# Four batches after the attention heads: three phases over all batches, or one chain per batch in two lanes

## The chip, the cores and the metric

One core of one Trainium2 chip runs the whole program. The metric is the device time of one execution in microseconds; the median of three runs of the kernel before is 2055.33 us (2053.5 to 2062.61). In the text PE is TensorE, DVE is VectorE, ACT is ScalarE, POOL is GpSimd and SP is the engine whose queue issues most DMAs.

## What is computed

The input is x of shape (4, 1024, 128) in float32: four batches of 1024 tokens. Four blocks follow one another, each on a layer-normed x (the norm has no weights):

```
x = x + L0_attn(norm(x))   # 16 heads of 8; a softmax and a second kernel of |S|, Wo, its own norm, + input
x = x + L0_ffn(norm(x))    # softmax gate over 8 experts, weights under 0.1 dropped, dense expert products
x = x + L1_attn(norm(x))   # one causal head of 64
x = x + L1_ffn(norm(x))    # soft decision tree: 255 sigmoids, 256 leaf probabilities, leaf values, Wout
```

L0_attn ends, once the heads' results f are there, with y = f Wo + bo, out = h + ln_w * normed(y) + ln_b, and x + out, where h is the normed x. The tree turns gates g into leaf probabilities level by level: for each of 8 levels every node's value is split into value * g and value - value * g. No block mixes tokens of different batches.

## The kernel before

`build` (L134) calls four functions in order, and each ends with a barrier of its own block, so that none of the next function's instructions starts before all of this one's are through: `attend_heads` (the heads, all four batches), `mix_experts` (y, its norm, the gate and the experts), `attend_causal` and `descend_tree`. x lives in SBUF as 32 tiles of 128 tokens by 128 (`x_res`), eight tiles a batch. Each engine runs its own list of instructions in the written order; semaphores connect them.

`attend_heads` works in slots, one tile of 128 keys of one head a slot, 512 slots in all. Besides, work that belongs to no slot (projections of the next batch, and once `prepare`, which turns and folds the weights of the later blocks) is laid between the slots at fixed places: a generator yields the slot at which its next piece is due, and the class `Beside` places it.

The three later functions go through the four batches with `rounds` (L121), which staggers parts of neighbouring batches by a fixed lead on each engine:

- `mix_experts` (L930): PE turns f and multiplies it by Wo, DVE adds bo (L1075), takes statistics and norms y (L1084), POOL multiplies by ln_w and adds to x (L1063, L1066). DVE norms x again (L1096), PE turns it (L1016), gate logits go through an exp on ACT (L990) and eight small DVE steps. The eight expert products of a tile come as two matmuls of 512 columns (L1032) in two PSUM banks; DVE adds each expert into x, weighted, with one instruction of 128x128 (L1142, 256 of them). Two tiles are taken in turn, so that an instruction waits for the one before the last.
- `attend_causal` (L1157): per tile of 128 queries, PE multiplies q by k (L1360), DVE adds the mask to the diagonal block (L1240), takes the maximum of each row (L1242) and scales it (L1246), ACT takes the exp (L1283), PE turns the weights (L1370), DVE copies them out of PSUM (L1234), PE weighs v (L1380), DVE divides (L1222), PE turns and ACT copies the result (L1278), PE projects it (L1392), DVE adds it to x (L1228). POOL adds the bias bo1 (L1323).
- `descend_tree` (L1411): norm (L896 and L898 on ACT: Ln and Exp; L1457 on DVE), turning (L1524), logits (L1532), sigmoids on ACT (L1498), 16 DVE instructions for the eight levels (L1469 to L1476, up to 128x1024), turning of the leaves (L1543), their copies (L1505), the product with the leaf values (L1549), the update of x (L1483) and the DMA to the output (L1559). POOL adds the bias (L1516).

Each of the three owns all eight PSUM banks while it runs. `take_stats` (L882), `take_rstd` (L893) and `four` (L918) are helpers that they share. The program has ACT load a set of function tables where a function is not in the loaded one; `attend_heads`, `mix_experts` and `attend_causal` load a set with both Ln and Exp by hand at their start, the rest is placed by the compiler.

## Time and profile before

| what | value |
|---|---|
| median of three runs | 2055.33 us |
| the profiled execution, its own time | 2054.09 us |
| its span in the profile | 2052.3 us |
| granted clock of TensorE, mean over the span | 0.933 of full |
| DVE busy | 1738.2 us (85%) |
| ACT busy | 1631.2 us (79%) |
| PE busy | 1578.5 us (77%) |
| POOL busy | 1406.9 us (69%) |
| DMA, mean | 16 GB/s |

The page divides the span into 40 slices of 51 us and gives the busy share of each engine in tenths. ACT and DVE stand at 9 from slice 4 to slice 31; in the last eight ACT has 1 to 4, POOL 0 or 1, and DVE falls from 8 to 5 or 6. The granted clock stands at 9 of 10 or better in the middle and at 7 or 8 in the end. A share is that of an average over stages, so the views that cut the span by stage are to be read beside it. Idle time of an engine is listed with what ended it; what counts is the idle time of the engine on which the end of the stage hangs.

### The profile page before, as it was taken

The page shows a single profiled execution, that of the slowest core. Times are in us where ns is not written, and L with a number is a line of the kernel's source. Part 1 is how long each engine was busy: PE and PEld are TensorE (multiplying, and loading weights), DVE is VectorE, ACT ScalarE, POOL GpSimd, SP SyncE. Part 2 cuts the span into 40 slices and gives each one's busy share as a digit, 9 for nine tenths or more (in the row PEclk, how much of TensorE's full clock was granted, in tenths as well). Part 3 has the DMA queues.
Part 4 walks back from the last instruction along what each step waited for, and adds up shares of the span by engine and source line. Part 5 has one row for each costly group of instructions (what it writes and reads, how often), then busy time and mean ns, then how long its engine had stood idle before and what let it go on. Part 6 is the DMA issues. An engine that isn't in the chain of part 4 may idle for free. (4 is left out here: it accounts for less than half of the span.)

```text
span 2052.3 us, 26693 instructions
## 1 busy us (share of the span) xinstructions
PE 1578.5 (77%) x8579; PEld 562.9 (27%) x8579; DVE 1738.2 (85%) x3742; ACT 1631.2 (79%) x1406; POOL 1406.9 (69%) x962
## 2 busy tenths in 40 slices
PE   2587787777878878778878887778777587899966
PEld 1122222222222222222222222222222144366655
DVE  3889999997999999879999999999998278755556
ACT  2689999998999999989999999999999411122243
POOL 2889889987999989788998989988998001000000
PEclk7799999999999999989999999999999888877788
DMA  4000000001000000010000000000000000000001
GB/s 113 27 28 13 13 14 17 13 13 31 25 13 13 13 16 15 9 40 13 18 13 13 13 15 16 12 13 13 18 13 7 1 0 1 1 1 1 0 1 42
DMA packets 32490, 33.11 MB, mean 16 GB/s; under 512 B 5657, under 2 KB 23136, under 8 KB 32352
## 3 DMA queue, kind: packets, MB, share of 16 engines
q1 hardware_dynamic: 31056, 31.06, 5.0%
q8 instruction: 71, 1.16, 0.2%
q14 instruction: 67, 0.55, 0.1%
q10 hardware_dynamic: 1296, 0.35, 0.1%
HBM read 22.74 MB, written 8.39 MB: 15 GB/s over the span
## 5 line engine op out<-in xcount | busy, mean ns | idle before, releaser
L879 POOL TENSOR_TENSOR sigma_weights<-grown 128x1024 f32<-128x1024 f32 x448 | 845.6, 1893 | 0.0
L792 ACT ACTIVATE tau_weights<-ps_tau 128x1024 f32<-128x1024 f32 x512 | 740.1, 1446 | 29.6 <-PE ps_tau L424 29.5
L573 DVE TENSOR_SCALAR sigma_weights<-ps_sig 128x512 int32<-128x512 int32 x1024 | 693.4, 677 | 81.3 <-PE ps_sig L415 80.3
L852 POOL TENSOR_SCALAR grown<-sigma_weights,kernel_shape 128x1024 f32<-128x1024 f32 x448 | 501.3, 1119 | 196.8 <-DVE sigma_weights L573 196.7
L778 ACT ACTIVATE sigma_weights<-sigma_weights,kernel_shape 128x2048 f32<-128x2048 f32 x256 | 621.0, 2426 | 0.0
L582 DVE TENSOR_TENSOR running_max<-ps_sig,running_max 128x512 f32<-128x512 f32 x896 | 606.0, 676 | 0.0
L787 ACT ACTIVATE sigma_weights<-sigma_weights 128x2048 f32<-128x2048 f32 x256 | 598.4, 2338 | 0.0
L466 PE MATMUL ps_acc<-sigma_weights,v_heads 128*9 128x512 f32 x2048 | 534.6, 601 | 0.0
L466 PE MATMUL ps_acc<-tau_weights,v_heads 128*9 128x512 f32 x2048 | 533.1, 600 | 0.4 <-DVE sums L599 0.3
L424 PE MATMUL ps_tau<-q_operand,k_operand 128*128 128x512 bf16 x1024 | 310.5, 385 | 262.7 <-ACT tau_weights L792 256.2
L415 PE MATMUL ps_sig<-q_operand,k_operand 96*128 96x512 bf16 x1024 | 400.6, 391 | 67.0 <-DVE running_max L582 41.3
L415 PEld LDWEIGHTS ps_sig<-q_operand,k_operand 96*128 96x128 bf16 x1024 | 99.2, 97 | 483.7 <-DVE running_max L582 287.2
L424 PEld LDWEIGHTS ps_tau<-q_operand,k_operand 128*128 128x128 bf16 x1024 | 63.9, 97 | 412.7 <-ACT tau_weights L792 343.7
L1323 POOL TENSOR_TENSOR x_res<-x_res,bo_rows 128x512 f32<-128x512 f32 x8 | 9.9, 1262 | 152.8 <-DVE z_c L1213 152.8
L466 PEld LDWEIGHTS ps_acc<-tau_weights,v_heads 128*9 128x9 f32 x2048 | 54.4, 88 | 193.9 <-issue 165.3
L1063 POOL TENSOR_TENSOR y_normed<-y_normed,ln_w_rows 128x1024 f32<-128x1024 f32 x4 | 9.4, 2342 | 138.0 <-DVE y_normed L1084 138.0
L783 ACT ACTIVATE sigma_weights<-sigma_weights,kernel_shape 128x1024 f32<-128x1024 f32 x64 | 100.6, 1573 | 0.0
L1032 PE MATMUL ps_me<-experts,turned_sb 128*128 128x512 f32 x128 | 74.8, 735 | 21.0 <-DVE x_res L1142 20.8
L586 DVE TENSOR_REDUCE row_max<-ps_misc 128x4 f32<-128x512 f32 x128 | 87.0, 680 | 2.0 <-PE ps_misc L433 2.0
L579 DVE COPY running_max<-ps_sig 128x512 f32<-128x512 f32 x128 | 87.0, 679 | 0.0
L433 PE MATMUL ps_misc<-ident,running_max 128*128 128x128 f32 x512 | 82.7, 286 | 4.1 <-DVE row_max L586 4.0
L1516 POOL TENSOR_TENSOR x_res<-x_res,bout_rows 128x512 f32<-128x512 f32 x8 | 10.0, 1268 | 104.4 <-DVE z_d L1457 104.4
(169 smaller groups left out, 1459.8 us busy)
## 6 DMA issues: line engine op xcount, KB each, us to landing
q_operand<-q_parts SPq DMA_DIRECT2D x192, 48.0 KB
k_operand<-k_parts SPq DMA_DIRECT2D x64, 144.0 KB
q_parts<-parts SPq DMA_DIRECT2D x24, 128.0 KB, 2.3
k_parts<-parts SPq DMA_DIRECT2D x24, 128.0 KB, 2.3
x_res<-in_L_attn_x SPq DMA_DIRECT2D x8, 256.0 KB, 5.3
q_operand<-max_rows SPq DMA_DIRECT2D x128, 2.0 KB
out<-x_res SPq DMA_DIRECT2D x4, 512.0 KB, 3.2
experts<-in_L_ffn_expert_w SPq DMA_DIRECT2D x1, 512.0 KB
```

What stands on the lines that cost most here:

```text
L415: pe.matmul(ps_sig[:, half, :], kop[0:SIGMA_ROWS, slot, keys], qop[0:SIGMA_ROWS, slot, half * HALF:(half + 1) * HALF], start=True, stop=Tr ...
L424: mm = pe.matmul(ps_tau[:, half, :], kop[:, head % SLOTS, of * P:(of + 1) * P], qop[:, head % SLOTS, half * HALF:(half + 1) * HALF], start ...
L466: mm = pe.matmul(ps_acc[32 * q:32 * q + COLS, :], v[:, (of - 1 + kind) % (2 * H), j, :], weights[:, half * HALF:(half + 1) * HALF], start= ...
L573: dve.tensor_scalar(sig[:, g % SIG_RING, cols].bitcast(I32), ps_sig[:, half, :].bitcast(I32), SIGN_OFF, None, ALU.bitwise_and).then_inc(ma ...
L579: dve.tensor_copy(run[:, of, cols], ps_sig[:, half, :]).then_inc(run_ready, 1)
L582: dve.tensor_tensor(run[:, of, cols], ps_sig[:, half, :], run[:, of, cols], ALU.max).then_inc(run_ready, 1)
L778: act.activation(chunk(c), chunk(c), ACT.Ln, bias=shape[:, CHUNK * c // TB % H, 1:2]).then_inc(ln_done, 1)
L783: act.activation(tile, tile, ACT.Square, bias=shape[:, g // TB % H, 0:1]).then_inc(whole_ready, 1)
L787: act.activation(chunk(c), chunk(c), ACT.Exp, scale=-1.0).then_inc(sig_done, 1)
L792: act.activation(tau[:, g % TAU_RING, :], ps_tau[:, :, :].rearrange("p h q -> p (h q)"), ACT.Exp, scale=float(DH) ** -0.5).then_inc(tau_do ...
L852: pool.tensor_scalar(grown[:, g % GROWN_RING, :], sig[:, g % SIG_RING, :], 1.0, shape[:, g // TB % H, 0:1], ALU.mult, ALU.add).then_inc(gr ...
L879: pool.tensor_tensor(sig[:, g % SIG_RING, :], t, t, ALU.mult).then_inc(sq_ready, 1)
```

## The change

The first function stays, with small additions. The three later ones are gone; in their place `finish_batches` writes for each batch b one chain per engine: y and its norm, gate, experts, causal attention, tree, output. Chains of batches 0 and 2 use the buffers and four PSUM banks of lane "even", 1 and 3 those of lane "odd". A chain is a generator that yields the time at which its next piece is due, counted from CHAIN * b = 60 * b; `together` merges the four generators of an engine into one list by due time. The due times decide the order of the instructions alone: nothing waits for a time. A piece that waits for a semaphore holds up what is behind it on its engine, of the other lane too. A use of a bank waits until the use four places earlier in the same lane was read.

Within the chain:

- The bias rows (bo, gate bias, expert biases, bv and bo1, bout) no longer are added by DVE or POOL. They stand as three bf16 parts in one 3-row tensor, and a matmul of ones with them opens the PSUM accumulation. `prepare` in `attend_heads` makes them: eleven small DVE instructions and five on one partition of 1544 elements, and two DMAs.
- Wo is centred over its columns beforehand, so that y has mean zero; the matmul gives y and y * ln_w side by side. ACT squares with a running sum, takes Ln and Exp per four tiles, and DVE adds y * ln_w * rstd to x in one instruction a tile. POOL has nothing to do after the heads.
- The expert updates of a tile follow one another, each waiting for the one before, in banks of their own (16 uses of 512 columns).
- Causal attention: maxima are taken of the scores by DVE (12 reductions), turned and copied as a row by a DMA into row 64 of q (k has ones there); then the scores are made a second time, keys on the partitions, with the maximum subtracted by the matmul; ACT takes 12 exps straight into the weights, so that these need no turning and no copy by DVE. The mask is added by a bf16 matmul. v is multiplied by wo1 beforehand and has a column of ones, so that the product gives the update and the sum of the weights; DVE takes the reciprocal and adds the update to x, one instruction a tile.
- Norms: DVE norms four tiles, ACT the other four (`Identity` with scale and bias).
- Tree: as before, without the bias on POOL. Each batch is stored in two halves.

The load of the table set at the start of the later functions is gone. The diff, cut to what the text speaks of:

```diff
-LATER = 22
+LATER, ROW32 = 17, 5
...
+SCORES = [(i, g) for i in range(TB) for g in range(1 + i // 4)]
+WEIGHTS = [(k, 0) for k in range(4)] + [(k, 1) for k in range(TB)]
+OUTS = [(0, 1), (2, 3), (4, 5, 6), (7,)]
+
+
+LANES, BANKS = 2, 4
+CHAIN = 60.0
...
+def turns():
+
+    names = ["f0", "f1", "y0", "y1", "y2", "y3", "z0", "z1", "gate"]
+    names += [f"e{i}" for i in range(2 * TB)]
+    names += ["c0", "c1", "q0", "k0", "q1", "k1", "v0", "v1"]
+    names += [f"s{i}" for i in range(12)] + ["m"]
+    names += [f"p{i}" for i in range(6)] + ["o0", "o1"] + [f"p{i}" for i in range(6, 12)] + ["o2", "o3"]
+    names += ["d0", "d1", "g0", "g1", "g2", "g3", "l0", "l1", "l2", "l3", "w0", "w1"]
+    return {name: n for n, name in enumerate(names)}
...
+def together(chains):
+
+    due = [(next(pieces), n) for n, pieces in enumerate(chains)]
+    while due:
+        at, n = min(due)
+        due.remove((at, n))
+        later = next(chains[n], None)
+        if later is not None:
+            due.append((later, n))
...
         attend_heads(nc, a, w)
-        mix_experts(nc, w)
-        attend_causal(nc, w)
-        descend_tree(nc, w, out)
+        finish_batches(nc, w, out)
...
+            def prepare(t0):
+                yield t0 + 4
...
+                yield t0 + 9
+                dve.wait_ge(row_step, 5)
+                dve.tensor_copy(rows3[0:1, :], rows32[:, :]).then_inc(split_step, 1)
+                yield t0 + 10
+                dve.wait_ge(split_step, 1)
+                dve.tensor_tensor(rows32[:, :], rows32[:, :], rows3[0:1, :], ALU.subtract).then_inc(split_step, 1)
+                yield t0 + 11
+                dve.wait_ge(split_step, 2)
+                dve.tensor_copy(split[:, 0, :], rows32[:, :]).then_inc(split_step, 1)
+                yield t0 + 12
+                dve.wait_ge(split_step, 3)
+                dve.tensor_tensor(rows32[:, :], rows32[:, :], split[:, 0, :], ALU.subtract).then_inc(split_step, 1)
+                yield t0 + 13
+                dve.wait_ge(split_step, 4)
+                dve.tensor_copy(split[:, 1, :], rows32[:, :]).then_inc(split_step, 1)
...
+class Lane:
...
+        self.banks = [ctx.enter_context(nc.psum_tensor(f"ps_{name}{i}", [P, HALF], F32)) for i in range(BANKS)]
...
+        self.reach = [self.weights[:, 4 * i:4 * i + 4, :].rearrange("p a c -> p (a c)").rearrange("p (t l) -> p t l", t=TB)
+                      for i in range(2)]
+        self.ready = [sem(f"bank{i}_ready") for i in range(BANKS)]
+        self.read = [sem(f"bank{i}_read") for i in range(BANKS)]
...
+def finish_batches(nc, w, out):
...
+                def biased(n, at, cols, row):
+                    pe.matmul(lane.bank(n)[:, at:at + cols], ones3[:, :], rows3[:, row:row + cols], start=True, stop=False)
...
+                for i in range(4):
+                    n = u(f"y{i}")
+                    yield t0 + 1.6 + 1.1 * i
+                    lane.was_read(pe, u(f"f{i // 2}"))
+                    lane.take(pe, n)
+                    for t in (2 * i, 2 * i + 1):
+                        at = t % 2 * 2 * D
+                        biased(n, at, 2 * D, ROW_Y)
+                        mm = pe.matmul(lane.bank(n)[:, at:at + 2 * D], zt[:, t * P:(t + 1) * P], w["woc"][:, :],
+                                       start=False, stop=True)
+                    done(mm, n)
...
+                for i in range(2 * TB):
+                    n, t, half = u(f"e{i}"), i // 2, i % 2
+                    yield t0 + (18.6 + 1.06 * i if i < 4 else expert_time(i - 3) + 0.2)
+                    lane.take(pe, n)
+                    biased(n, 0, HALF, ROW_E + half * HALF)
+                    done(pe.matmul(lane.bank(n)[:, :], zt[:, t * P:(t + 1) * P], w["experts"][:, 4 * half:4 * half + 4, :],
+                                   start=False, stop=True), n)
...
+                for j in range(12):
+                    yield t0 + 72.8 + 1.05 * j + (2.2 if j >= 6 else 0)
+                    weights(j)
+                    if j == 5:
+                        yield t0 + 78.9
+                        weigh(0)
+                        yield t0 + 79.6
+                        weigh(1)
+                yield t0 + 88
+                weigh(2)
+                yield t0 + 92
+                weigh(3)
...
+                def layer_norm(norm, at):
+                    z0 = 3 * r + norm
+                    yield t0 + at
+                    dve.wait_ge(lane.stats_ready, TB * (z0 + 1))
+                    alone(dve, w["dve_passed"])
+                    for t in range(TB):
+                        dve.bn_aggr(lane.mv[:, t, :], lane.stats[:, t, :]).then_inc(lane.mv_ready, 1)
+                    yield t0 + at + 2
+                    dve.wait_ge(lane.rstd_ready, z0 + 1)
+                    dve.scalar_tensor_tensor(out=lane.shift[:, :], in0=lane.mv[:, :, 0], scalar=-1.0, in1=lane.rstd[:, :],
+                                             op0=ALU.mult, op1=ALU.mult).then_inc(lane.shift_ready, 1)
+                    dve.wait_ge(lane.mv_ready, TB * (z0 + 1))
+                    for t in range(4):
+                        ins = dve.tensor_scalar(lane.z[:, t, :], xt(b, t), lane.mv[:, t, 0:1], lane.rstd[:, t:t + 1],
+                                                ALU.subtract, ALU.mult)
+                    ins.then_inc(lane.z_ready[0], 1)
...
+                for i in range(2 * TB):
+                    n, t = u(f"e{i}"), i // 2
+                    for s in range(4):
+                        yield t0 + expert_time(i) + 0.35 * s
+                        e = 4 * (i % 2) + s
+                        if s == 0:
+                            if i == 0:
+                                dve.wait_ge(lane.gate_step, step + 9)
+                            lane.arrived(dve, n)
+                            if i % 2:
+                                lane.was_read(dve, u(f"e{i - 1}"))
+                        else:
+                            dve.wait_ge(lane.e_step, 3 * (2 * TB * r + i) + s)
+                        ins = dve.scalar_tensor_tensor(out=xt(b, t), in0=lane.bank(n)[:, s * D:(s + 1) * D],
+                                                       scalar=lane.weight[:, t, e:e + 1], in1=xt(b, t),
+                                                       op0=ALU.mult, op1=ALU.add)
+                        if s < 3:
+                            ins.then_inc(lane.e_step, 1)
+                        else:
+                            done(ins, n)
+                    if i % 2:
+                        yield t0 + expert_time(i) + 1.45
+                        lane.was_read(dve, n)
+                        stat(t)
...
+                def squares(i):
+                    n = u(f"y{i}")
+                    lane.arrived(act, n)
+                    for t in (2 * i, 2 * i + 1):
+                        centred = lane.bank(n)[:, t % 2 * 2 * D:t % 2 * 2 * D + D]
+                        ins = act.activation(centred, centred, ACT.Square, accum_out=lane.y_sum[:, t:t + 1])
+                    ins.then_inc(lane.sum_ready, 1)
+
+                def take_y_rstd(g):
+                    cols = slice(4 * g, 4 * g + 4)
+                    act.wait_ge(lane.sum_ready, 4 * r + 2 * g + 2)
+                    act.activation(lane.y_ln[:, cols], lane.y_sum[:, cols], ACT.Ln, bias=w["eps"][:, 0:1], scale=1.0 / D)\
+                        .then_inc(lane.yln_ready, 1)
+                    act.wait_ge(lane.yln_ready, 2 * r + g + 1)
+                    act.activation(lane.y_rstd[:, cols], lane.y_ln[:, cols], ACT.Exp, scale=-0.5).then_inc(lane.y_rstd_ready, 1)
...
+                yield from layer_norm(TREE, 96.9)
+                for g in range(2):
+                    yield t0 + 99.8 + 0.8 * g
+                    copy_turned(u(f"d{g}"), g)
+                for i in range(4):
+                    n = u(f"g{i}")
+                    yield t0 + 102.4 + 0.9 * i
+                    lane.arrived(act, n)
+                    done(act.activation(lane.right[:, 2 * i:2 * i + 2, 0:NODES],
+                                        lane.bank(n)[:, :].rearrange("p (t n) -> p t n", t=2)[:, :, 0:NODES], ACT.Sigmoid), n)
...
+            together([chain(b, CHAIN * b) for b in range(B)])
```

## Rows read from the trace of the kernel before

**Rows 1.** The windows view: length, busy us (instructions) of five engines, granted clock, DMA share, GB/s.

```profile
40.00:1619.50 1579.50, 1232.54 (x7088) 330.73 (x7089) 1445.40 (x2695) 1509.32 (x1154) 1357.08 (x920) 0.97 0.06 17
1619.50:1779.80 160.30, 116.14 (x416) 65.14 (x416) 123.63 (x508) 19.70 (x45) 18.75 (x8) 0.81 0.00 1
1779.80:1965.70 185.90, 164.33 (x752) 115.07 (x752) 99.72 (x340) 53.03 (x129) 9.93 (x8) 0.78 0.00 1
1965.70:2052.30 86.60, 54.30 (x288) 44.92 (x288) 55.23 (x168) 38.00 (x58) 9.97 (x8) 0.84 0.09 25
```

**Rows 2.** The windows view of a stretch inside the heads.

```profile
240.00:400.00 160.00, 127.26 (x754) 33.32 (x754) 154.22 (x285) 160.00 (x119) 143.68 (x99) 1.00 0.04 14
```

**Rows 3.** The view of waits after 1619.5: who waited for whom, us, times, longest.

```profile
ACT prob_c L1283 <- DVE shift_c L1246: 34.1, 29, 3.8
...
DVE v_c L1258 <- PE ps_cx L1347: 27.0, 4, 7.1
DVE mixed L1222 <- PE ps_co L1380: 26.7, 11, 3.9
```

**Rows 4.** The view of groups by form after 1619: count, busy us, mean ns, idle.

```profile
L1142 DVE SCALAR_TENSOR_TENSOR x_res<-ps_me,gate_weight,x_res 128x128 f32<-128x128 f32 x256 | 68.3, 341 | 6.5 <-PE ps_me L1032 6.4
...
L1234 DVE COPY prob_t<-ps_ct 128x512 f32<-128x512 f32 x24 | 16.3, 684 | 2.9 <-PE ps_ct L1370 2.9
...
L1505 ACT ACTIVATE reach_t<-ps_dl 128x512 f32<-128x512 f32 x16 | 9.3, 596 | 21.9 <-PE ps_dl L1543 21.8
```

**Rows 5.** The timeline from 1642 to 1650: gate and first expert updates; start, duration, what.

```profile
1642.19 3.51 PE L1022 MATMUL ps_my<-gate,turned_sb 128*128 128x8 f32 x16
...
1648.84 1.40 DVE L1142 SCALAR_TENSOR_TENSOR x_res<-ps_me,gate_weight,x_res 128x128 f32<-128x128 f32 x5
```

**Rows 6.** The timeline from 1965.7 to 1984: norms, table loads, a held level.

```profile
1965.76 1.64 DVE L886 BATCH_NORM_STATS2 stats_d<-x_res 128x6 f32<-128x128 f32 x8 [0.54 <-PEq L1164]
1967.55 0.64 DVE L890 BATCH_NORM_AGGREGATE mv_d<-stats_d 128x2 f32<-128x6 f32 x8
1968.22 0.30 ACT L896 ACTIVATE lnv_d<-mv_d,eps 128x8 f32<-128x8 f32 x1 [4.24 <-DVE mv_d L890]
1968.56 0.21 ACT L898 ACTIVATE rstd_d<-lnv_d 128x8 f32<-128x8 f32 x1
1968.88 2.14 DVE L1457 TENSOR_SCALAR z_d<-x_res,mv_d,rstd_d 128x128 f32<-128x128 f32 x8 [0.69 <-ACT rstd_d L898]
...
1973.30 1.28 ACT L1498 ACT_TABLE_LOAD   x1 [1.12 <-PE ps_dg L1532]
...
1978.02 1.28 ACT L896 ACT_TABLE_LOAD   x1
1979.32 0.30 ACT L896 ACTIVATE lnv_d<-mv_d,eps 128x8 f32<-128x8 f32 x1
1979.64 1.28 ACT L898 ACT_TABLE_LOAD   x1
...
1983.57 1.18 DVE L1474 TENSOR_TENSOR reach<-reach,right 128x16 f32<-128x16 f32 x1
```

**Rows 7.** The timeline from 1747 to 1755: the gate matmuls again.

```profile
1751.63 1.91 PE L1022 MATMUL ps_my<-gate,turned_sb 128*128 128x8 f32 x16
```

**Rows 8.** The timeline from 2033 to the end: levels of the last tree, last update.

```profile
2033.56 0.18 DVE L1474 TENSOR_TENSOR reach<-reach,right 128x16 f32<-128x16 f32 x1 [0.17 <-DVE reach L1470]
...
2035.62 0.43 DVE L1474 TENSOR_TENSOR reach<-reach,right 128x256 f32<-128x256 f32 x1
2036.08 0.43 DVE L1476 TENSOR_TENSOR reach<-reach 128x256 f32<-128x256 f32 x1
...
2039.26 1.23 DVE L1476 TENSOR_TENSOR reach<-reach 128x1024 f32<-128x1024 f32 x1
```

**Rows 9.** The DMA issues of the page: KB each, median us from issue to landing.

```profile
q_parts<-parts SPq DMA_DIRECT2D x24, 128.0 KB, 2.3
...
out<-x_res SPq DMA_DIRECT2D x4, 512.0 KB, 3.2
```

## What the change is predicted to do

> **What bounds the kernel now.** I read the windows by stage first. From 40 to 1619.5 us ACT is busy 1509 of 1580 us and DVE 1445 [rows 1]; in an undisturbed stretch ACT has 160.0 of 160 and DVE 154.3 [rows 2]. The heads are bound by ACT, with DVE 4% behind. The reader is to see that the other three stages are of another kind: experts 160.3 us, causal 185.9, tree 86.6, together 432.8 us, with DVE busy 123.6, 99.7 and 55.2 (278.6 in all), PE 334.8 and ACT 110.7 [rows 1]. In the causal stage no engine but PE is near full, and PE only because its clock is 0.78: the waits there go round, ACT for DVE's maximum, DVE for PE's product [rows 3]. A tile runs through all three engines and two tiles are in flight. What the change can win is this waiting and the DVE work that it drops, within 433 us.
>
> **The heads.** The chain code starts after the same barrier, so the heads count in full. New there is DVE work for the bias rows. No row shows an instruction on one partition of 1544 elements; the nearest is the level of 1024 elements, 1.23 us [rows 8], which gives 1.8 us each and 9 for the five; if the three that only copy went at double speed it would be 6. Eleven small ones by 0.2 us add 2. DVE's slack is 4%, 0.12 us in a slot of 3.05, and PE's next scores wait for DVE, so little of a delay is absorbed where five such come in consecutive slots; but ACT is the bound and lies behind DVE. Ends: 0 and 11 us; I take 6, since the slack before them is about what two slots hide. The added POOL work at the start lies before POOL has anything to do, and PE's and ACT's additions are five instructions under 0.5 us: nothing. SP issues as many loads as before; its two row DMAs at slot 38 wait for DVE's last split, and behind them stand the operand loads, three heads ahead: nothing, or 2 us if that lead is used up.
>
> **What a chain asks of DVE.** An update of 128x128 from PSUM lasts 0.34 us, but five start within 1.40, so one every 0.26 [rows 4, 5]. One that waits for the one before starts after its duration and 0.03 more (0.43 to 0.46) [rows 8]: 0.37. Statistics take 1.64 for eight, aggregation 0.64, a norm 0.26 a tile [rows 6]. So per batch: y update 8 by 0.26 = 2.1; statistics three times 1.6 = 4.9; aggregation 1.9; norm 12 by 0.26 and three shifts = 3.6; gate nine by 0.25 = 2.3; experts 64 by 0.37 = 23.7; k and the last update, four by 0.6 = 2.4; 12 maxima over 36 blocks of 128, by 0.6 for a full bank (0.68 long, as the copy [rows 4]) = 5.7; outputs 2.9; levels, two each of 0.17, 0.18, 0.20, 0.23, 0.29, 0.43, 0.69, 1.23 and the gaps = 7.2 (the 1.18 of a small level beside POOL is gone [rows 6, 8]). Sum 57, four chains 227 against 279. Dropped are the copies of turned weights (24 of 0.68 and the shorter ones), mask, divisions, bias adds and half the norms. The one thing dearer is the experts: 0.37 for 0.26, 7 us a batch, because each now follows its predecessor.
>
> **Table loads.** ACT takes Sigmoid from another set than Ln and Exp. In the tree stage every batch after the first loads for Ln (1978.02), again for Exp (1979.64) and again for Sigmoid, 1.28 us each [rows 6]; until the first Sigmoid there is none. The set loaded for Ln doesn't hold Exp; whether the one loaded for Exp holds Ln is shown nowhere, as a Sigmoid always stood between. Bounds: no load for such an Ln, or 1.28. I take 1.28, since the two were placed in one way. In the merged order the first Sigmoid is at due time 102; after it come 12 pairs of Ln and Exp and three more Sigmoids: 28 loads with the first. A norm whose way from the aggregation to the first normed tile was 0.68 us (1968.20 to 1968.88) then takes 3.2. This is a price without a pause behind the load. The Trainium skill, ScalarE: Activation LUTs, What ACT_TABLE_LOAD costs, adds about 1.38 us of drain to each switch, 2.66 in all. Here the Ln starts 0.02 us after its load ends [rows 6], so the measurement decides; by the skill's page the sum below would be an estimated 29 us higher.
>
> **The path, lane by lane.** Alone (first chain), from the start to the first maximum: turning f and copying 1.2; y matmuls and eight squares with sums to 5.9, rsqrt to 6.9; update, statistics, aggregation to 9.5; norm to 11.3; turning, copy (0.60 [rows 4]), gate matmuls (16 in 1.91 at full clock [rows 7]) to 14.7; gate 3.3, to 18; experts 23.7 and eight statistics 1.9, to 43.6; norm 2.5; turning, q, k, v 4.7: 51. Alone (last chain), from the first maximum: maxima 5.8; turning, copy and the row DMA 3.2 (2.3 from issue to landing of a larger one [rows 9]), to 9; exps over 4608 columns at the rate of the copies to 15; outputs to 19.2; norm with two loads 5.1; turning and logits 1.8; load and sigmoids 3.4; levels 7.2; leaves, product and last update 4.4: 41. Then 3.2 us to landing [rows 9] and issue: 3.5.
> Between them stand three slots in which the first half of one chain meets the second half of the one before, in DVE's written order. Until the experts start: maxima, y, statistics, norm, gate and two outputs are 16 us of work, but DVE waits for ACT's rsqrt, for the norm, for turning and for the gate's exp: 25 us without loads, 31.5 with (2.6 for the first rsqrt, 1.3 for the second, which the maxima half cover, 2.6 for the norm). Experts: 23.7 and 1.9, and 4.4 of the other chain's outputs and norm, less 1.5 that fills gaps: 28.5, with loads 29.5. From there to the next maximum: two levels and aggregation 1.4, norm with loads 3.2 and 1.2, remaining levels 4.9 (while PE makes q and k), leaves and product before v and the first score in PE's order 4.8: 15.5. So the second slot is 69, the third and fourth 76.5. DVE works 57 of each and waits for the rest.
>
> **The clock.** The three stages ran at 0.81, 0.78 and 0.84 granted: 32 to 44% of the time at 1.2 GHz, and the same 16 gate matmuls took 3.51 us at the low level and 1.91 at the high [rows 1, 5, 7]. The low level comes where PE has waited, and in the chains PE's work on the path (turning, gate, q, k, leaves) stands just behind such waits. About 10 us of it lie in each of the five parts; doubling 38% of it gives 19. PE's share of work is larger in the chains, which speaks for fewer such stretches; ends 0 and 19, I take 12.
>
> **Sum.** Tail: 51 + 69 + 76.5 + 76.5 + 41 + 3.5 + 12 = 329.5 us for 432.8. Span: 1619.5 + 6 + 329.5 = 1955. The profiled execution took 1.8 us more than its span, and the median is 1.2 above it: 1958.
>
> **Rivals.** (1) The slots take what their order was written for, 60 us each and 121 from start to end of a chain: 301 + 3.5 + 12 of clock, hence 1945 as the median; without the clock term 1933. For it: DVE's 57 us fit. Against it: each Ln to Exp way has 1.6 us in the order and takes up to 3.7.
> (2) The set that Exp loads serves Ln too: in the third and fourth slot only the loads after a Sigmoid stay, 7.5 us less in each: 1943. The Trainium skill, ScalarE: Activation LUTs, Table sets, has one set with both and counts one load for Ln then Exp, while the rows show two; by it the loads were seven, and the time this one.
> (3) PE stays at 1.2 GHz throughout. Its work per chain is 39 us at the high level (experts 10, scores twice 9, weighing 4, leaves and logits 6, the rest 10), 78 at the low: it becomes the bound of a slot, with the 12 us in which it waits 90, and the ends 20 longer: 1619.5 + 6 + 51 + 270 + 41 + 20 + 3.5 and the 3 us to the median, 2014. Against it: 0.97 in the heads.
> (4) The lanes don't run side by side: a wait of one chain at the head of PE's or DVE's list holds the other until both are serial: 4 by 92 and loads of 30 and 19 of clock: 420, or 2049, no change. It decides if a slot takes over 95 us.
> (5) The other side: serial as in (4), and PE at the low level all along because it idles between steps, which adds 25 us to each chain: 500 us and 2130. It decides where the tail passes 427. Against it: experts of one chain have no PSUM bank, buffer or semaphore of the other, and 28 us of PE work beside them.
> (6) ACT pauses behind each load: 21 of the 28 lie on the path. With the pause of the Trainium skill (ScalarE: Activation LUTs, What ACT_TABLE_LOAD costs) that is an estimated 1987. Against it: the 0.02 us between load and Ln [rows 6].
>
> **Chances.** Forecast 0.45, (1) 0.18, (2) 0.11, (3) 0.09, (4) 0.05, (5) 0.03, (6) 0.05; the rest, 0.04, is below all. The range takes in the heads' 0 to 11, the clock's 0 to 19 and (1), (2), (6): 1925 to 1995. A measurement tells 0.5% from no change, 10 us. Faster 0.95, same 0.02, slower 0.03.
>
> **What would show it.** Right: the span's tail between 315 and 345; 28 table loads, 12 of them before an Ln; expert updates starting every 0.37 us; DVE busy about 230 us in the tail with its waits on ACT's rsqrt and norm; second slot shorter than the third by 6 to 9 us, read from one chain's first expert update to the next one's. Wrong: DVE's waits lying elsewhere (on PE's experts, or on the other lane), a heads stage longer by over 11 us, or a clock under 0.75 in the tail.

## The result, and the profile after

The changed kernel takes 2122.32 us (median of 4, 2120.69 to 2138.47); the kernel before, beside it, takes 2055.51. The ratio is 1.034, with a 95% interval of 1.028 to 1.039: slower by 3.4%, where 4.7% faster was forecast. The profiled execution has a span of 2118.9 us.

The windows view of after, in stretches of the tail (the chains' part, from 1635.2 us on). Columns as in [rows 1]: length, busy us of PE, PEld, DVE, ACT, POOL with their instructions, granted clock, DMA share, GB/s.

```profile
1635.00:1700.00 65.00, 48.87 (x142) 21.61 (x142) 37.23 (x132) 13.13 (x42) 0.00 (x0) 0.82 0.00 0
1700.00:1760.00 60.00, 56.25 (x157) 33.21 (x158) 13.63 (x48) 12.49 (x40) 0.00 (x0) 0.52 0.00 0
1760.00:1820.00 60.00, 52.78 (x225) 29.82 (x224) 39.77 (x140) 20.51 (x37) 0.00 (x0) 0.94 0.00 1
1820.00:1880.00 60.00, 55.81 (x218) 34.17 (x218) 25.74 (x89) 22.16 (x51) 0.00 (x0) 0.83 0.03 9
...
1635.20:2118.90 483.70, 413.86 (x1572) 246.44 (x1572) 222.90 (x766) 147.88 (x316) 0.00 (x0) 0.80 0.02 5
```

The first thing to see is PE: it is busy 53 to 56 of 60 us wherever two chains stand side by side, 414 of 484 in all. In the stages before, it was 335 of 433 [rows 1]. DVE is less than half busy, and fell from 279 us to 223, as it was meant to. The second thing is the clock: 0.52 from 1700 to 1760 while PE is busy throughout.

So the time went to two places. The heads end at 1635.2 instead of 1619.5: 15.7 us. The tail takes 483.7 us instead of 432.8: 51 us more, where 103 less was forecast.

The timeline of after in the experts of the first chain (start, duration, what, how many records):

```profile
1661.88 0.39 PE L1095 MATMUL ps_even<-bias_rows,ones 3*128 3x512 bf16 x1
1662.20 1.12 PE L1130 MATMUL ps_even<-experts,z_turned_even 128*128 128x512 f32 x2
1663.26 0.39 PE L1095 MATMUL ps_even<-bias_rows,ones 3*128 3x512 bf16 x1
1663.57 1.13 PE L1130 MATMUL ps_even<-experts,z_turned_even 128*128 128x512 f32 x2
```

One expert bank is one bias matmul and one fp32 matmul. The fp32 one stands as x2: **each fp32 matmul is two records**. From bank to bank it is 1.37 us, the distance of the bias matmuls. Before, the same thing could be read from a count: line 1032 runs 64 times and has 128 records,

```profile
L1032 PE MATMUL ps_me<-experts,turned_sb 128*128 128x512 f32 x128 | 74.8, 735 | 21.0 <-DVE x_res L1142 20.8
```

Who waited for whom on PE in the tail of after (us in total, times, longest):

```profile
PE ps_even L1087 <- DVE z_even L1288: 20.3, 3, 8.5
PE ps_odd L1087 <- DVE z_odd L1288: 16.7, 3, 5.9
PE ps_odd L1246 <- DVE causal_weights_odd L1424: 8.0, 1, 8.0
PE ps_even L1185 <- DMA causal_q_even<-causal_max_rows_even: 4.8, 2, 2.7
PE ps_odd L1185 <- DMA causal_q_odd<-causal_max_rows_odd: 4.3, 2, 2.1
```

With the smaller waits that is about 70 us in all: norms that the other chain doesn't cover, the levels of the last tree, and the rows of the maxima.

**A budget of the 414 us.** From the records one can add up the start-to-start distances, and separately what the columns alone take (0.43 us for 512 fp32 columns in one record at the full clock, twice for a matmul; half of 0.43 for bf16). Columns alone: 254 us. The same records' distances, with the parts at the half clock halved (that is, the work as it would be at 2.4 GHz, "at full" below): 330. As they were: 414. So beyond the columns 76 us lie between matmuls and 84 in the clock. The experiments take these apart.

### The profile page after: what moved, and what is told of

It reads as the page before. It is cut to its first block and busy times, and to the rows that moved or that the text cites. A ratio compares the mean times of both kernels' runs of the same rounds, so it can differ in the third digit from the quotient of the medians.

```text
span 2118.9 us, 26652 instructions
## 1 busy us (share of the span) xinstructions
PE 1669.7 (79%) x8700; PEld 585.7 (28%) x8700; DVE 1696.1 (80%) x3507; ACT 1669.6 (79%) x1493; POOL 1371.5 (65%) x944
## 5 line engine op out<-in xcount | busy, mean ns | idle before, releaser
L881 ACT ACTIVATE tau_weights<-ps_tau 128x1024 f32<-128x1024 f32 x512 | 725.3, 1417 | 42.6 <-PE ps_tau L463 42.5
L867 ACT ACTIVATE sigma_weights<-sigma_weights,kernel_shape 128x2048 f32<-128x2048 f32 x256 | 613.4, 2396 | 0.0
L876 ACT ACTIVATE sigma_weights<-sigma_weights 128x2048 f32<-128x2048 f32 x256 | 590.9, 2308 | 0.0
L472 PEld LDWEIGHTS ps_misc<-ident,running_max 128*128 128x128 f32 x512 | 66.6, 147 | 30.7 <-DVE running_max L663 12.7
L685 DVE COPY sums<-ps_acc 128x512 f32<-128x512 f32 x65 | 44.3, 682 | 20.3 <-PE ps_acc L505 20.3
L505 PEld LDWEIGHTS ps_acc<-sigma_weights,v_heads 128*9 128x9 f32 x2048 | 54.5, 89 | 3.5 <-issue 2.3
L1364 DVE SCALAR_TENSOR_TENSOR x_res<-ps_odd,gate_weight_odd,x_res 128x128 f32<-128x128 f32 x128 | 44.4, 347 | 6.8 <-PE ps_odd L1130 2.0
```

The costliest lines, as they stand in the source:

```text
L472: mm = pe.transpose(ps_misc[:, t * P:(t + 1) * P], run[:, head % 2, q:q + P], ident[:, :])
L505: mm = pe.matmul(ps_acc[32 * q:32 * q + COLS, :], v[:, (of - 1 + kind) % (2 * H), j, :], weights[:, half * HALF:(half + 1) * HALF], start= ...
L867: act.activation(chunk(c), chunk(c), ACT.Ln, bias=shape[:, CHUNK * c // TB % H, 1:2]).then_inc(ln_done, 1)
L876: act.activation(chunk(c), chunk(c), ACT.Exp, scale=-1.0).then_inc(sig_done, 1)
L881: act.activation(tau[:, g % TAU_RING, :], ps_tau[:, :, :].rearrange("p h q -> p (h q)"), ACT.Exp, scale=float(DH) ** -0.5).then_inc(tau_do ...
```

## The experiments

Every run is timed beside the kernel before (2055.5 to 2056.4 us in the four sets). "Tail" is from the turning of the first f to the end of the profiled span. PE's distances "at full" are as in the budget. Later edits build on earlier ones, which is said.

**Without the biases.** The bias matmuls are left out, and with them the making of their rows in the heads.

```
-                        biased(n, at, 2 * D, ROW_Y)
-                    biased(n, 0, HALF, ROW_E + half * HALF)
...
-                dve.tensor_copy(rows3[0:1, :], rows32[:, :]).then_inc(split_step, 1)
-                dve.tensor_tensor(rows32[:, :], rows32[:, :], rows3[0:1, :], ALU.subtract).then_inc(split_step, 1)
...
```

> Leaves out every bias that the change folds into rows: the 192 three-row bf16 matmuls of the chains, and the making of the rows in the heads stage (the single-partition reductions, the split into three parts, its two copies). Theory A, TensorE's work sets the tail (every fp32 matmul is two records, 330 us of work at the full clock, 414 with the clock as granted): the 42 us that the bias matmuls occupy go from the tail, which takes 435 to 450 us instead of 484, and the heads stage ends near 1624 instead of 1635; 2060 to 2080 us in all. Theory B, the chain of norms, table loads and single waits sets the tail: only the 11 us of the heads go, about 2110. Theory C, the order written out sets it: also about 2110.

Measured: 2025.1 us, ratio 0.986 (0.984 to 0.987). The heads end at 1620.1, the tail takes 402 us. The direction is theory A's, but the tail lost 82 us, not 34 to 49. PE's distances at full fell from 330 to 269: 61 us, of which the bias matmuls' own are 38. The rest fell at their neighbours: expert matmuls 65.7 to 61.4, y 19.8 to 16.0, leaves 20.2 to 14.7, v 13.2 to 7.5. A bias matmul makes the matmul behind it dearer too. The time at 1.2 GHz fell as well, from 194 to 130 us.

The heads' part is settled by it, as far as one trace can: without the row operations only 0.6 us of 15.7 is left. (Heads of one and the same code end some us apart from trace to trace: 1619.5 in the kernel before, 1623.4 in its variant further down.) These are the operations of after on DVE in that stretch (mean ns and count; the bar is followed by busy us):

```profile
L642 DVE CAST bias_split<-bias_rows 1x1544 bf16<-1x1544 f32 x1 | 2.6, 2640 | 0.0
L623 DVE TENSOR_TENSOR bias_rows<-bias_rows,ln_w_rows 1x128 f32<-1x128 f32 x1 | 2.0, 1972 | 0.0
L618 DVE TENSOR_SCALAR bias_rows<-bias_row,bo_mean 1x128 f32<-1x128 f32 x1 | 1.9, 1942 | 0.0
L633 DVE TENSOR_TENSOR bias_rows<-bias_rows 1x1544 f32<-1x1544 f32 x1 | 1.8, 1837 | 0.0
L639 DVE TENSOR_TENSOR bias_rows<-bias_rows,bias_split 1x1544 f32<-1x1544 f32 x1 | 1.8, 1837 | 0.0
L636 DVE CAST bias_split<-bias_rows 1x1544 bf16<-1x1544 f32 x1 | 1.6, 1587 | 0.0
L630 DVE CAST bias_rows<-bias_rows 1x1544 bf16<-1x1544 f32 x1 | 0.9, 942 | 0.0
```

They add up to 12.8 us, 13.5 with three small ones, and the heads were 15.7 late: nothing of it was absorbed. Why the same kind of operation lasts so differently can be seen where GpSimd's work is laid beside it (the timeline, start and duration first):

```profile
151.35 1.89 POOL L975 TENSOR_TENSOR sigma_weights<-grown 128x1024 f32<-128x1024 f32 x1
151.37 1.94 DVE L618 TENSOR_SCALAR bias_rows<-bias_row,bo_mean 1x128 f32<-1x128 f32 x1
...
166.12 0.94 DVE L630 CAST bias_rows<-bias_rows 1x1544 bf16<-1x1544 f32 x1
...
182.42 1.89 POOL L975 TENSOR_TENSOR sigma_weights<-grown 128x1024 f32<-128x1024 f32 x1
182.49 2.64 DVE L642 CAST bias_split<-bias_rows 1x1544 bf16<-1x1544 f32 x1
```

The operation of 128 elements ends 0.08 us after GpSimd's, beside which it began. The cast takes 0.94 us where GpSimd did nothing, and ends 0.81 us after GpSimd's where it began beside one. So in these places DVE stood until GpSimd was through; this is read from the order in time, no run tests it.

**One table set.**

```
                                         lane.bank(n)[:, :].rearrange("p (t n) -> p t n", t=2)[:, :, 0:NODES], ACT.Sigmoid), n)
+                act.preload_act_table_set("natural_log_exp_and_others")
```

> Keeps in ScalarE one table set that holds both Ln and Exp; it is changed only for the four groups of sigmoids, so 8 loads of 1.28 us stand in the tail instead of 28. Theory A (TensorE's work sets the tail): the 26 us taken from ScalarE and from the norms are mostly covered by the other chain's matmuls, the tail shortens by 0 to 10 us, 2112 to 2122. Theory B (norms and loads are on the path, as the prediction had them): 24 to 30 us less, about 2095.

Measured: 2113.05 us median, but 2088.28 to 2120.47 over four executions; ratio 1.024 (1.017 to 1.031), which overlaps that of after. ACT's busy time in the tail fell from 148 to 123 us, the tail by 11. Theory B's 24 to 30 us did not appear. The size is not settled by this run, since the half-clock time fell by 20 us as well (194 to 174), and its stretches lie elsewhere: none of 58 us from 1702 on, but one of 61 us from 1913 on, in the third chain.

**Full rows in the scores.**

```
-        self.q, self.k = sb("causal_q", [DA + 1, N]), sb("causal_k", [DA + 1, N])
+        self.q, self.k = sb("causal_q", [P, N]), sb("causal_k", [P, N])
...
-                        mm = pe.matmul(lane.bank(n)[:, 0:cols - P * diagonal], q[0:DA, i * P:(i + 1) * P],
+                        mm = pe.matmul(lane.bank(n)[:, 0:cols - P * diagonal], q[0:96, i * P:(i + 1) * P],
...
+                dve.memset(lane.k[DA:96, :], 0.0).then_inc(lane.ones_set, 1)
+                dve.memset(lane.k[96:P, :], 1.0).then_inc(lane.ones_set, 1)
```

> Queries and keys of causal attention stand in tiles of 128 partitions, zeros in the rows added, the row maxima in row 96: the first scores have 96 rows in place of 64, the second 128 in place of 65; everything else as after. Theory D (the granted clock falls where matmuls of 64 rows run back to back, 58 us at the half clock from 1702 to 1760): that stretch is at the full clock, the scores take 0.22 to 0.24 us each instead of up to 0.43 and the tail is 20 to 35 us shorter, 2088 to 2102. Rival (the clock falls for another reason): within 5 us of after, 2117 to 2127.

Measured: 2069.15 us, ratio 1.007 (1.005 to 1.009): 53 us less than after, with not one column or instruction of PE's less. The direction is theory D's, the gain well beyond its 20 to 35 us. The tail takes 431.6 us. The windows view of a stretch of 58 us, after first (1702.5 on), then this run (1699.7 on):

```profile
1702.50:1760.50 58.00, 54.25 (x147) 32.01 (x147) 14.06 (x51) 11.70 (x39) 0.00 (x0) 0.50 0.00 0
```

```profile
1699.70:1757.70 58.00, 53.28 (x236) 33.57 (x234) 28.39 (x101) 14.54 (x45) 0.00 (x0) 0.89 0.00 1
```

PE is busy alike in both, but does 236 matmul records where it did 147. At full, the distances fell by 4 us only (330 to 326); nearly all of the gain is the clock: the time at 1.2 GHz in the tail fell from 194 to 102 us.

**Half of the expert columns.**

```
-                    done(pe.matmul(lane.bank(n)[:, :], zt[:, t * P:(t + 1) * P], w["experts"][:, 4 * half:4 * half + 4, :],
+                    done(pe.matmul(lane.bank(n)[:, 0:2 * D], zt[:, t * P:(t + 1) * P], w["experts"][:, 4 * half:4 * half + 2, :],
```

> TensorE makes only 256 of the 512 columns of each expert matmul (the bias matmul still covers 512, so the other half of the outputs are the bias alone); VectorE's updates, all waits and all buffers are unchanged. Theory A (TensorE sets the tail): the expert matmuls occupy 35 us instead of 70, the tail is 25 to 35 us shorter, 2087 to 2097. Rival, the prediction's (VectorE's updates of 0.34 us pace the experts): nothing changes, 2120 to 2124.

Measured: 2102.23 us, ratio 1.023 (1.021 to 1.024), the tail 20 us shorter. PE's expert work at full fell by 29 us (65.7 to 37.0), but the time at 1.2 GHz rose from 194 to 219 us. The rival ("nothing changes") is refuted, the size missed by 5 us: part of the gain was given back in clock.

**The kernel before with full rows in its scores.**

```
-        qk = sb("qk_c", [DA, 2, N])
+        qk = sb("qk_c", [P, 2, N])
...
+            pool.memset(qk[DA:P, :, :], 0.0).then_inc(pads, 1)
```

> The kernel before with one edit: its queries and keys of causal attention stand in a tile of 128 partitions, the upper 64 zero, so that its score matmuls have 128 rows in place of 64. No lanes, no folded biases. Theory D (matmuls of few rows leave the granted clock low): the half-clock stretches of 24 us in the causal stage of before (at 1812, 1860 and 1908) go, some 7 to 12 us each, 2015 to 2040 us. Rival (in after it was the lanes' mixture, not the rows): 2050 to 2060.

Measured: 2057.13 us, ratio 1.000 (0.999 to 1.001). Theory D missed. The half-clock stretches of 23.9 us are all there, and the causal stage has its 185.9 us and 0.78 again:

```profile
1783.60:1969.50 185.90, 162.80 (x752) 116.57 (x752) 99.96 (x342) 52.73 (x129) 11.36 (x9) 0.78 0.00 1
```

So few rows in the scores alone don't keep the clock low. That turned the question from the rows to their changes. In the order of the records, a matmul of up to 64 rows and one of more follow each other 104 times in the tail of before (72 of them are left in this run), 448 times in that of after, and still 384 times with full rows in the scores: twice for each bias matmul.

**128 rows in every matmul** (built on the full rows in the scores).

```
-        w["rows3"] = sb("bias_rows", [PARTS, ROWS], BF16)
-        w["ones3"] = sb("ones3", [PARTS, P], BF16)
+        w["rows3"] = sb("bias_rows", [P, ROWS], BF16)
+        w["ones3"] = sb("ones3", [P, P], BF16)
...
+            pool.memset(rows3[:, :], 0.0).then_inc(rows_clear, 1)
```

> The run with full rows in the scores (2069 us, tail 431.5, 104 us of it at the half clock) and beside it the bias matmuls with 128 rows in place of 3: the ones and the bias rows stand in tiles of 128 partitions, the other 125 zero. The same columns, the same count. Theory D: the stretches at the half clock that are left shrink by 20 to 50 us and the tail by 5 to 20, 2050 to 2065. Rival (a bias matmul costs what its columns and its place between fp32 matmuls make it cost, whatever its rows): 2065 to 2073.

Measured: 2026.41 us, ratio 0.986 (0.984 to 0.987): 43 us less again, far beyond theory D's 5 to 20, and now below the kernel before. No change between up to 64 rows and more is left. The tail takes 389.0 us (ten records of bias matmuls are missing from this trace, some 2 us). Its windows view, and the timeline in the experts:

```profile
1637.20:2026.20 389.00, 307.21 (x1562) 210.51 (x1572) 225.46 (x770) 146.99 (x316) 0.00 (x0) 0.89 0.02 6
```

```profile
1665.30 0.38 PE L1098 MATMUL ps_even<-bias_rows,ones 128*128 128x512 bf16 x1
1665.51 1.02 PE L1133 MATMUL ps_even<-experts,z_turned_even 128*128 128x512 f32 x2
1666.37 0.38 PE L1098 MATMUL ps_even<-bias_rows,ones 128*128 128x512 bf16 x1
1666.59 1.02 PE L1133 MATMUL ps_even<-experts,z_turned_even 128*128 128x512 f32 x2
```

From bank to bank 1.07 us instead of 1.37, which is 0.15 us for each of the two changes. 1.07 is what the columns take, and nothing else. Over the whole tail PE's distances at full fell from 326 to 280 us by 384 changes fewer, so **each change between 3 and 128 rows had cost 0.12 us on average**. The time at 1.2 GHz fell by 19 us only (102 to 83).

Where at least a part of this is lost shows in the weight loads (PEld). In after the load stands just before its matmul; here it starts as soon as the matmul before has started, 0.43 us ahead of its own, and is covered:

```profile
1663.25 0.09 PEld L1095 LDWEIGHTS ps_even<-bias_rows,ones 3*128 3x128 bf16 x1 [0.76 <-issue]
1663.26 0.39 PE L1095 MATMUL ps_even<-bias_rows,ones 3*128 3x512 bf16 x1
```

```profile
1665.94 0.10 PEld L1098 LDWEIGHTS ps_even<-bias_rows,ones 128*128 128x128 bf16 x1 [0.24 <-issue]
1666.37 0.38 PE L1098 MATMUL ps_even<-bias_rows,ones 128*128 128x512 bf16 x1
```

**The bias rows alone** (scores left at 64 and 65 rows).

> The kernel after with one edit: the bias matmuls have 128 rows in place of 3; the scores keep their 64 and 65. Theory E (a matmul that has fewer rows than the one before or after it costs 0.1 us more at each change, and 384 of these changes are the bias matmuls'): TensorE's work falls by some 46 us at the full clock, the tail by 45 to 75, 2050 to 2075 us. Rival (the gain of the two row edits needed both, the clock being what counts): above 2095.

The edit is the one just shown, made in after. Measured: 2056.15 us, ratio 0.999 (0.998 to 1.000), 66 us less than after, inside theory E's range. Distances at full 290 (40 us less), time at 1.2 GHz 135 us (60 less), tail 420. The two row edits thus bring 66 and 53 us alone and 96 together.

**64 rows, then 65** (in the run with 128 rows everywhere).

```
-                    pe.matmul(lane.bank(n)[:, at:at + cols], ones3[:, :], rows3[:, row:row + cols], start=True, stop=False)
+                    pe.matmul(lane.bank(n)[:, at:at + cols], ones3[0:64, :], rows3[0:64, row:row + cols], start=True, stop=False)
```

> The run with 128 rows in all matmuls (2026 us) with the bias matmuls over 64 of the rows. Theory E in its narrow form (what costs is that one matmul takes half of the array's rows or fewer and its neighbour all): the 0.1 us at each change is back, 2050 to 2072 us. Rival (what costs is the very small number, 3; or the clock follows the rows in proportion): at most half of the 43 us comes back, 2026 to 2047.

> The run before with one row more: the bias matmuls over 65 of the 128 rows, against 64 (2069 us) and 128 (2026 us). Theory E in its narrow form (up to half of the array's rows beside matmuls of all rows cost 0.1 us at each change, more than half cost nothing): 2022 to 2032 us. Rival (the cost falls with the rows in proportion): 2050 to 2068.

Measured: 64 rows 2069.34 us, 1.006 (1.005 to 1.008); 65 rows 2027.57 us, 0.986 (0.985 to 0.988). One row more is worth 42 us. The timeline with 64 rows has the distances of after:

```profile
1667.96 0.39 PE L1098 MATMUL ps_even<-bias_rows,ones 64*128 64x512 bf16 x1
1668.28 1.13 PE L1133 MATMUL ps_even<-experts,z_turned_even 128*128 128x512 f32 x2
1669.34 0.39 PE L1098 MATMUL ps_even<-bias_rows,ones 64*128 64x512 bf16 x1
```

So a step it is, between 64 and 65 rows. The Trainium skill (TensorEngine Tiling (Array Packing), Key Properties) says that changing between tiling modes drains TensorE, and lists modes of 128, 64 and 32 rows. The runs agree that such a change costs time: with 3 and 64 rows 0.12 us at each change, with 65, 96 and 128 nothing. That a mode of 64 rows is what TensorE was in is not shown; the step between 64 and 65 fits it.

**Rows on GpSimd and one table set** (built on 128 rows everywhere): the table set kept as above, and the bias rows made by GpSimd.

```
-                dve.tensor_copy(rows3[0:1, :], rows32[:, :]).then_inc(split_step, 1)
...
+                pool.tensor_copy(rows3[0:1, :], rows32[:, :]).then_inc(split_step, 1)
...
```

> As the run before this one, and two edits more: ScalarE keeps the table set that holds Ln and Exp, and in the heads stage GpSimd makes the bias rows and their split instead of VectorE (all but the mean). Theory A with the heads' part by VectorE alone: the heads end at 1621 to 1625 instead of 1633 to 1635, since GpSimd has idle time there and VectorE has none; of the loads 0 to 8 us; so 10 to 20 us below the run before this one, 2032 to 2055. Rival for the heads (GpSimd's single-partition operations hold up its own squares, or stop VectorE at their shared port): the heads end near 1633 still.

Measured: 2018.74 us, ratio 0.983 (0.981 to 0.984), 8 us less, short of the 10 to 20 forecast. The heads end at 1628.6; in the three profiles with the rows on GpSimd it was 1625.8 to 1628.6, in the ten with the rows on DVE 1632.6 to 1638.8. So 4 us at least and some 8 in the middle of the 15.7 are won, less than thought; one operation of 1.94 us stayed on DVE. The tail lost 3.7 us by 20 table loads fewer. Spread over the loads that is 0.2 us each, where the prediction had 1.28 on the path for most. A few us either way between two single traces are not told apart.

**VectorE's work in the experts halved** (built on 128 rows everywhere).

```
+                        if s in (1, 2):
+                            continue
                         ins = dve.scalar_tensor_tensor(out=xt(b, t), in0=lane.bank(n)[:, s * D:(s + 1) * D],
```

> The run with 128 rows in all matmuls (2026 us, tail 389), and VectorE leaves out two of the four expert updates of every bank: 128 operations of 0.34 us, 44 us of VectorE's work in the tail, so half of the experts are missing from the result. Theory A (TensorE sets the tail): 0 to 12 us shorter, 2014 to 2026. The prediction's theory (VectorE's 57 us of each chain are the bound): about 40 us shorter, near 1986.

Measured: 2011.8 us, ratio 0.979 (0.977 to 0.980), the tail 375 us: 14 less for 42 us of DVE work. That is just past theory A's range and a third of what the other theory demands. DVE isn't the bound even in this faster version, though it isn't free: with all updates, PE waits 8.9 us in 15 places for one to release a bank, without the half of them 1.7.

**Chains further apart: 90 and 121.** 90 in the run with full rows in the scores, 121 in the version with 128 rows, the rows on GpSimd and the table set kept:

```
-CHAIN = 60.0
+CHAIN = 90.0
```

> The run with full rows in the scores (2069 us, tail 431.5) with the planned distance between chains 90 in place of 60, so that one chain stands alone in a third of the order. Theory A (TensorE's work sets the tail and two chains side by side only fill its waits): the stretches with one chain leave TensorE idle, the tail is 10 to 40 us longer, 2080 to 2110. Rival C (the order written for 60 makes the lanes wait for one another, since a slot takes 80 to 110 us, not 60): the tail is 5 to 25 us shorter, 2045 to 2064.

> The fastest version so far (128 rows, table set kept, rows on GpSimd; 2019 us, tail 385) with the planned distance between chains 121 in place of 60: the lanes run one after the other. Theory A (two chains side by side fill TensorE's waits, and these are most of what the change can bring): each chain stands alone with its own waits and takes 110 to 125 us, the tail 440 to 500, 2075 to 2130 us. Rival (the lanes bring little, since TensorE's work is the same): under 2045.

Measured: 2127.21 us, 1.034 (1.031 to 1.036), 58 more than its base and worse than theory A's range; and 2112.85 us, 1.028 (1.026 to 1.030), 94 more than its base. In turn, each chain takes 120 us of the 481, and PE waits for the norms (the waits on PE; compare 20.3 and 16.7 in after):

```profile
PE ps_even L1097 <- DVE z_even L1300: 37.4, 6, 8.4
PE ps_odd L1097 <- DVE z_odd L1300: 35.7, 6, 8.4
PE ps_odd L1258 <- DVE causal_weights_odd L1436: 16.1, 2, 8.0
PE ps_even L1258 <- DVE causal_weights_even L1436: 16.0, 2, 8.0
```

The lanes do what the change says: side by side they are worth 94 us. Some 28 of these are clock, since the time at 1.2 GHz rose from 80 to 161 us, and PE's work in it from 54 to 111.

**Chains closer: starts at 0, 45, 120, 165** (all edits so far).

```
-            together([chain(b, CHAIN * b) for b in range(B)])
+            together([chain(b, 120.0 * (b // 2) + 45.0 * (b % 2)) for b in range(B)])
```

> The fastest version so far (128 rows, table set kept, rows on GpSimd; 2019 us, tail 385) with chains planned to start at 0, 45, 120 and 165 instead of 0, 60, 120 and 180. Theory A (TensorE sets the pace where two chains stand side by side, and is idle where one stands alone, at the start and at the end): 15 us of the plan less alone, the tail 3 to 15 us shorter, 2004 to 2016. Rival C (the stages that now meet want the same engine at the same time): 2019 to 2035.

Measured: 1992.1 us, ratio 0.969 (0.967 to 0.970), 27 us less, past theory A's range. It is the fastest kernel here, 64 us below the kernel before. Two windows of its tail:

```profile
1660.00:1700.00 40.00, 33.04 (x149) 18.70 (x150) 26.63 (x96) 13.04 (x43) 0.00 (x0) 0.87 0.00 1
1700.00:1760.00 60.00, 56.36 (x263) 35.80 (x262) 38.61 (x139) 19.74 (x39) 0.00 (x0) 0.94 0.00 1
```

From 1700 to 1760 PE is as busy as in after, at 0.94 instead of 0.52, with 263 matmul records where after had 157. The tail is 365 us, 56 of it at 1.2 GHz. Why it won 27 us and not 15 isn't settled: the plan has 15 us less alone, and the half-clock time fell by 24 us.

## Why the prediction was wrong

**The failed step is TensorE's work, in the third rival: "Its work per chain is 39 us at the high level (experts 10 ...)".** It took one record of 0.43 us for a matmul of 512 fp32 columns. There are two. The columns alone are 63.4 us per chain (254 for four), and with what lay between matmuls 82.6 (330). By part, per chain and at full: experts 16.4 without their biases, scores 17.9 for both times (put at 9), weighing 8.2 (put at 4). With 83 in place of 39, PE's work alone is longer than every slot of the forecast, and DVE's 57 is not the bound. The path "lane by lane" is the wrong sum then: it follows DVE's order and lets PE's work lie beside it at no cost. Four times 82.6 alone is what was forecast for the whole tail. It could have been read from [rows 5]: the gate of one batch is eight matmuls in the code and x16 in the row. And by [rows 1] PE was busy 334.8 us in the stages before, so that a change that adds matmuls while it forecasts a tail of 329.5 needs an account of where PE's time goes. The Trainium skill has the same figure (FP8 and Floating Point Precision, TensorE Precision Notes): a true fp32 product is four passes of the array. The trace agrees: 2 by 0.43 us against 0.215 for as many bf16 columns.

**How far this step carries.** With 82.6 and the 12 us of waiting a slot is 94.6, three are 284 in place of 222, and the forecast's own sum becomes an estimated 2020: still faster than before. So the count alone does not make the loss. The runs divide the 164 us of the miss in two. With full rows in every matmul the kernel takes 2026, 68 above the forecast: that is PE's true work, and the heads. The other 96 are what the two row edits took away: 50 us of PE's work at full (330 to 280) and some 57 us in the clock (84 to 27), together a little more than the time that they bring. The forecast had nothing for the first and 12 us for the second, and they are what turned a gain into a loss.

**The folded biases** were costed in the heads only. In the tail they are 192 matmuls. Their columns are 21 us, and the 384 changes of rows 40 to 46 more (330 against 290 us, 326 against 280). With them the tail also spends 19 to 60 us more at 1.2 GHz (83 against 102 us, 135 against 194). "What the change can win is this waiting and the DVE work that it drops" left out that DVE's bias adds had moved to PE, the engine with the least room.

**The clock.** Forecast 12 us; the 414 us contain 84. The granted clock of the tail, 0.80, is no lower than before (0.78 to 0.84 [rows 1]), so the "under 0.75" warning didn't fire. But half a clock costs its full price only on the engine that is the bound. The step named as the cause (PE waiting before its work) fits most of the short stretches. It does not fit the two longest: the one of 58 us began 12 us after PE's last wait, and the one of 37.5 us (from 2037 on) after 18 us without a wait; PE was busy 94% and 91% in them. Both begin with the first scores of a chain, over 64 rows. In the runs with either row edit and the chains at 60 or closer no stretch is longer than 21 us.

**The heads.** Forecast 6, ends 0 and 11, measured 15.7: outside, and over the 11 us named as a sign of being wrong. The mechanism was right, two sizes were off. The five operations of 1544 elements took 8.8 us, as the upper figure had it (9). Two of 128 elements took 1.94 and 1.97 us instead of 0.2, beside operations of GpSimd. And the slack that the 6 us counted on absorbed nothing; without the operations the heads were at 1620.1.

**What held.** DVE's work: 222.9 us for 227 forecast, against 278.6. Updates start every 0.386 us at the median (0.37 forecast). The 28 table loads are there: 8 and 8 for the norms' Ln and Exp, 4 and 4 for y's, 4 for Sigmoid, 1.283 us each.

```profile
L1454 ACT ACT_TABLE_LOAD x8 | 10.3, 1283 | 0.3
L1456 ACT ACT_TABLE_LOAD x8 | 10.3, 1283 | 0.1
L1536 ACT ACT_TABLE_LOAD x4 | 5.1, 1283 | 0.1
```

In the forecast 21 of the 28 stood on the path, 27 us; 20 taken away gave 3.7 us where the clock stayed alike (79 and 83 us at 1.2 GHz). So most of a load costs nothing here, which fits that it lies beside the other chain's matmuls; no run puts a load alone.

**The slots.** Forecast 69, 76.5 and 76.5. From one chain's first expert update to the next chain's it is 103.1, 107.3 and 107.2 us, the first of them shorter by 4 where 6 to 9 was forecast:

```profile
1659.96 1.51 DVE L1364 SCALAR_TENSOR_TENSOR x_res<-ps_even,gate_weight_even,x_res 128x128 f32<-128x128 f32 x4
...
1763.09 3.11 DVE L1364 SCALAR_TENSOR_TENSOR x_res<-ps_odd,gate_weight_odd,x_res 128x128 f32<-128x128 f32 x8
...
1870.37 3.10 DVE L1364 SCALAR_TENSOR_TENSOR x_res<-ps_even,gate_weight_even,x_res 128x128 f32<-128x128 f32 x8
...
1977.54 3.10 DVE L1364 SCALAR_TENSOR_TENSOR x_res<-ps_odd,gate_weight_odd,x_res 128x128 f32<-128x128 f32 x8
```

**The rivals.** (1), (2), (4) and (6) gave times below 2050 and fell. (3) named the right engine with half of its work: 2014. With 82.6 in place of 39 its own slots, at 1.2 GHz throughout, would be 177 us and its sum an estimated 2275; the tail's clock was 0.80, not half. (5) gave 2130, near 2122, by a mechanism that isn't there: the lanes are not serial, and in turn they cost 94 us more. A right number with a wrong mechanism is a miss too. The range of 1925 to 1995 and the 0.95 for faster rested on one reading, PE's 39 us per chain: (3) and (5) varied its clock, and no rival varied the 39 itself or gave a price to a change of rows.

## What to carry to other kernels

Before a path is added up by waits, add up each engine's work for the new program, and count a matmul's records against the matmuls that the code issues. Here that one count took two thirds of the forecast gain, by the estimate above. Moving work from an engine that is half idle to the one with the least room costs its full price: 61 us of PE's work for the biases. Matmuls of 64 rows or fewer in turn with full ones are dear; zeros up to 65 rows or more take that away at no cost in columns, and here this alone decides between a loss (2122 us) and a gain (2026).

## What had not been expected of the hardware

- A change between matmuls of at most 64 rows and of 128 rows costs 0.12 us each way on average (280 against 327 us for 384 changes), 0.15 between the banks of the experts, and none with 65 rows. At such a change the weight load is no longer covered by the matmul before.
- PE's clock was at 1.2 GHz for 58 us in which PE was busy for 54. With the rows of the scores filled up it was at 0.89 there. In the kernel before, filling them up changed nothing (its stretches of 23.9 us stayed). Without any bias matmul and with scores of 64 rows the longest stretch was 27 us, after 18 us of unbroken work. What makes the clock fall in busy work stays open.
- Operations of DVE on one partition lasted 0.36 to 1.97 us for 128 elements and 0.94 to 2.64 us for 1544, the same cast three times at 0.94, 1.59 and 2.64. Those of 1.94, 1.97, 1.59 and 2.64 us began beside an operation of GpSimd and ended 0.08 to 0.81 us after it; the cast of 0.94 us had none beside it. GpSimd made the two subtractions in 3.1 us each and the casts in 1.46 each time.
